# Sums of weight blocks at the start of a Winograd-form product: GpSimd arithmetic replaced by ScalarE negations and accumulating DMAs

## The reference, cut to what matters

```python
# x: (128, 64, 1024); all float32
h   = gelu(cond @ W0 + b0); h = gelu(h @ W1 + b1)
att = softmax(h @ W2 + b2)                                   # (128, 8)
y   = einsum('boi,bih->boh', einsum('bk,koi->boi', att, weight), x) + (att @ bias_k)[:, :, None]
base   = einsum('bsd,od->bso', y, base_W)                    # (1024, 1024) weights
probs  = softmax(einsum('bsd,ed->bse', y, router_W))         # 8 experts, top 2, renormalised
mid    = einsum('bsd,edr->bser', y, lora_A) * w_dense[..., None]
out    = x + base + einsum('bser,erd->bsd', mid, lora_B) * 2
```

## Time and profile before

| | |
|---|---|
| time, median of 3 (lowest, highest) | 975.08 us (975.04, 975.86) |
| profiled execution's own time | 974.32 us |
| span of its instructions | 972.6 us |
| TensorE busy | 953.3 us |
| VectorE busy | 762.2 us |
| ScalarE busy | 231.6 us |
| GpSimd busy | 328.1 us |
| mean granted TensorE clock | 0.995 of full |

### The profile page before, as it was taken

How to read it: one execution, slowest core, us unless ns; L and a number is a source line. 1 busy time by engine, 2 the same in 40 slices (tenths; PEclk the granted TensorE clock), 3 DMA queues, 4 the chain that set the end, 5 groups by cost and what they waited for, 6 DMA issues and landing times.

```text
span 972.6 us, 17914 instructions
## 1 busy us (share of the span) xinstructions
PE 953.3 (98%) x5747; PEld 878.0 (90%) x5747; DVE 762.2 (78%) x1650; ACT 231.6 (24%) x537; POOL 328.1 (34%) x247
## 2 busy tenths in 40 slices
PE   8789999999999999999999999999999999999998
PEld 6679999999999999999999999999999999999996
DVE  6998787777787777787777787777787777787774
ACT  4442222221222221222221222221222221222210
POOL 5833313333313333312333312333312333312331
PEclk9989999999999999999999999999999999999999
DMA  8243433323433323433323433323432323433311
GB/s 302 71 136 93 136 112 111 109 96 113 135 110 111 117 88 113 135 112 109 114 91 113 135 113 108 124 81 113 135 117 104 119 86 113 135 118 103 129 48 47
DMA packets 45969, 110.73 MB, mean 114 GB/s; under 512 B 20352, under 2 KB 20480, under 8 KB 45440
## 3 DMA queue, kind: packets, MB, share of 16 engines
q1 hardware_dynamic: 45680, 110.49, 34.8%
q10 hardware_dynamic: 272, 0.03, 0.0%
HBM read 76.92 MB, written 33.59 MB: 114 GB/s over the span
## 4 chain that ended last, share of the span: by engine, by line
PE 94%; DVE 5%; issue 1%; ACT 0%; POOL 0%; DVEq 0%; POOLq 0%; ACTq 0%
PE pc L511 17%; PE pa L522 13%; PE pb L522 13%; PE y_ps L483 11%; PE pb L525 10%; PE pa L525 10%; PE pd L511 9%; PE pd L566 4%; PE pc L566 4%; DVE w_lo L901 1%; PE pd L548 1%; PE pd L556 1%; DVE a_lo L997 0%; DVE b_lo L1123 0%; DVE ya L988 0%
## 5 line engine op out<-in xcount | busy, mean ns | idle before, releaser
L420 POOL TENSOR_TENSOR out_sb<-out_sb,u 128x512 f32<-128x512 f32 x93 | 132.1, 1449 | 208.4 <-DVE u L1083 208.4
L483 PE MATMUL y_ps<-mix_w,x_sb 128*128 128x128 f32 x1024 | 194.6, 274 | 0.2
L483 PEld LDWEIGHTS y_ps<-mix_w,x_sb 128*128 128x128 f32 x1024 | 167.8, 190 | 13.1 <-DVE ya L988 0.8
L390 POOL TENSOR_TENSOR ya<-ya 128x512 f32<-128x512 f32 x31 | 42.2, 1361 | 400.3 <-DVE ya L988 400.3
L988 DVE TENSOR_TENSOR ya<-y_ps,bias_sb 128x512 f32<-128x512 f32 x128 | 87.8, 686 | 35.6 <-PE y_ps L483 31.6
L511 PE MATMUL pc<-w_hi,s_hi 128*128 128x512 f32 x248 | 102.4, 413 | 0.0
L522 PE MATMUL pa<-w_hi,a_hi 128*128 128x376 f32 x248 | 97.8, 394 | 0.7 <-ACT p L821 0.7
L511 PE MATMUL pc<-w_hi,s_lo 128*128 128x512 f32 x248 | 97.5, 393 | 0.0
L511 PE MATMUL pc<-w_lo,s_hi 128*128 128x512 f32 x248 | 96.9, 391 | 0.0
L813 ACT ACTIVATE mid_hi<-pd 128x128 fp32r<-128x128 f32 x64 | 17.8, 278 | 282.7 <-PE pd L556 282.7
L806 ACT ACTIVATE exps<-logits,neg_max 128x8 f32<-128x8 f32 x64 | 19.3, 301 | 271.7 <-DVE neg_max L1005 271.7
(11 more groups left out here) (218 smaller groups left out, 2567.1 us busy)
## 6 DMA issues: line engine op xcount, KB each, us to landing
x_sb<-in_x SPq DMA_DIRECT2D x64, 512.0 KB, 3.9
out_sb<-in_x SPq DMA_DIRECT2D x64, 512.0 KB, 4.4
out<-out_sb SPq DMA_DIRECT2D x64, 512.0 KB, 2.7
bias_sb<-bias_rows SPq DMA_DIRECT2D x62, 64.0 KB, 4.8
a_raw<-in_base_t SPq DMA_DIRECT2D x1, 1024.0 KB, 7.6
b_raw<-in_base_t SPq DMA_DIRECT2D x1, 1024.0 KB, 11.9
c_raw<-in_base_t SPq DMA_DIRECT2D x1, 1024.0 KB, 13.0
w_raw<-in_base_t SPq DMA_DIRECT2D x1, 1024.0 KB, 14.8
```

The lines of the kernel that those rows point to most:

```text
L390: nc.gpsimd.tensor_tensor(y_block(0, 1), y_block(0, 1), y_block(0, 0), ALU.subtract).then_inc(s3_set, 1)
L420: nc.gpsimd.tensor_tensor(o, o, u2[:, :], ALU.add).then_inc(done, 1)
L483: mm = nc.tensor.matmul(y_ps[q % 2][:, j * P:(j + 1) * P], x_sb[m][:, c * P:(c + 1) * P], mix_w[m][:, :], start=True, stop=True)
```

## The change

B11 and B21 are loaded straight into the places of T2 and T4 in `w_raw`, and B12 is loaded two more times, into the places of T3 and T1, by two further 1 MiB loads in SyncE's queue ahead of `lora_b`. ScalarE writes the negative of a block into one of two buffers `neg[0]`, `neg[1]` (each 1 MiB, over the space of the operands S3, S2 and S1, S4), in two pieces of 128x1024, and a DMA issued by GpSimd adds the buffer to the block (`add_to`, `accum_op=ALU.add`): T3 = B12 + (-B22), T1 = B12 + (-B11), T2 = B11 + (-T3), T4 = B21 + (-T2). Each such DMA moves 1 MiB from SBUF to SBUF. Eight ScalarE negations of 128x1024 are added, the 16 GpSimd instructions go. `neg[0]` holds -B11 and then -T3, `neg[1]` -B22 and then -T2, so each buffer is written anew only after the add that read it. The lists of ScalarE and VectorE in `first_pair` are put in another order: T3's low part after the negation of T3; S3's high and low parts, T1's and T2's parts later; VectorE's waits for T1, T3 and T2 ahead of B12's and B22's low parts go. In ScalarE's list `exponents(0)` comes ahead of the wait for T3, and `exponents(1)` stands behind the waits for T3 and T1. GpSimd's `sum_s3` stands behind the add into T2, and `sum_s2` behind that into T4.

The diff, without the removal of three helpers and one constant that nothing else uses:

```diff
@@ -122,8 +121,9 @@
         lb_raw = over("lb_raw", D, lb_lo_at)
-        a_raw = over("a_raw", BLOCK, op_at[S3])
-        b_raw = over("b_raw", BLOCK, op_at[S1])
+        a_raw = w_raw[:, T2 * BLOCK:(T2 + 1) * BLOCK]
+        b_raw = w_raw[:, T4 * BLOCK:(T4 + 1) * BLOCK]
+        neg = [over(f"neg{n}", BLOCK, op_at[o]) for n, o in enumerate((S3, S1))]
         c_raw = over("c_raw", BLOCK, out_at[1])
...
@@ -166,7 +166,9 @@
             "params_in", "mix_i_in", "bk_in", "side_in", "lb_in"))
-        a_in, b_in, c_in, d_in = (sem(n) for n in ("a_in", "b_in", "c_in", "d_in"))
+        a_in, b_in, c_in, d_in, t1_in, t3_in = (sem(n) for n in ("a_in", "b_in", "c_in", "d_in", "t1_in", "t3_in"))
+        neg_b11_set, neg_b22_set, neg_t3_set, neg_t2_set = (sem(n) for n in (
+            "neg_b11_set", "neg_b22_set", "neg_t3_set", "neg_t2_set"))
         zeros_set, consts_set, pick_set = sem("zeros_set"), sem("consts_set"), sem("pick_set")
...
@@ -261,13 +259,15 @@
             sp.dma_start(bk_sb[:, :], bias_k).then_inc(bk_in, 16)
-            sp.dma_start(a_raw[:, :], base_t[0, :, :]).then_inc(a_in, 16)
+            sp.dma_start(a_raw, base_t[0, :, :]).then_inc(a_in, 16)
             sp.dma_start(x_sb[0][:, :], x_t[0, :, :]).then_inc(x_in[0], 16)
...
             sp.dma_start(x_sb[1][:, :], x_t[1, :, :]).then_inc(x_in[1], 16)
-            sp.dma_start(b_raw[:, :], base_t[2, :, :]).then_inc(b_in, 16)
+            sp.dma_start(b_raw, base_t[2, :, :]).then_inc(b_in, 16)
             sp.dma_start(c_raw[:, :], base_t[1, :, :]).then_inc(c_in, 16)
             sp.dma_start(d_raw, base_t[3, :, :]).then_inc(d_in, 16)
+            sp.dma_start(w_raw[w_block(T3)], base_t[1, :, :]).then_inc(t3_in, 16)
+            sp.dma_start(w_raw[w_block(T1)], base_t[1, :, :]).then_inc(t1_in, 16)
             sp.dma_start(lb_raw[:, :], lora_b.rearrange("e r d -> (e r) d")).then_inc(lb_in, 16)
...
@@ -348,41 +348,15 @@
             for n in range(WP):
-                nc.gpsimd.tensor_copy(w_hi[w_piece(B11, n)], a_raw[half_block(n)]).then_inc(w_hi_set[B11], 1)
+                nc.gpsimd.tensor_copy(w_hi[w_piece(B11, n)], w_raw[w_piece(T2, n)]).then_inc(w_hi_set[B11], 1)
             for n in range(WP):
                 pool.wait_ge(w_hi_set[B11], n + 1)
-                nc.gpsimd.tensor_tensor(w_lo[w_piece(B11, n)], a_raw[half_block(n)],
+                nc.gpsimd.tensor_tensor(w_lo[w_piece(B11, n)], w_raw[w_piece(T2, n)],
                                         w_hi[w_piece(B11, n)].bitcast(f32), ALU.subtract).then_inc(w_lo_set[B11], 1)
 
-            def make_t1(n):
-                nc.gpsimd.tensor_tensor(w_raw[t_piece(T1, n)], c_raw[quarter(n)], a_raw[quarter(n)],
-                                        ALU.subtract).then_inc(t1_made, 1)
-
-            def make_t3(n):
-                nc.gpsimd.tensor_tensor(w_raw[t_piece(T3, n)], c_raw[quarter(n)], w_raw[t_piece(B22, n)],
-                                        ALU.subtract).then_inc(t3_made, 1)
-
-            def make_t2(n):
-                pool.wait_ge(t1_made, n + 1)
-                nc.gpsimd.tensor_tensor(w_raw[t_piece(T2, n)], w_raw[t_piece(B22, n)], w_raw[t_piece(T1, n)],
-                                        ALU.subtract).then_inc(t2_made, 1)
-
-            def make_t4(n):
-                pool.wait_ge(t2_made, n + 1)
-                nc.gpsimd.tensor_tensor(w_raw[t_piece(T4, n)], b_raw[quarter(n)], w_raw[t_piece(T2, n)],
-                                        ALU.subtract).then_inc(t4_made, 1)
-
-            pool.wait_ge(c_in, 16)
-            for n in range(TP):
-                make_t1(n)
-            pool.wait_ge(d_in, 16)
-            for n in range(TP):
-                make_t3(n)
-            for n in range(TP):
-                make_t2(n)
-            pool.wait_ge(b_in, 16)
-            for n in range(TP):
-                make_t4(n)
+            def add_to(blk, of, done):
+
+                nc.gpsimd.dma_start(w_raw[w_block(blk)], neg[of][:, :], accum_op=ALU.add).then_inc(done, 16)
 
...
@@ -420,7 +394,19 @@
             def first_pair():
+                pool.wait_ge(t3_in, 16)
+                pool.wait_ge(neg_b22_set, WP)
+                add_to(T3, 1, t3_made)
+                pool.wait_ge(t1_in, 16)
+                pool.wait_ge(neg_b11_set, WP)
+                add_to(T1, 0, t1_made)
+                pool.wait_ge(w_lo_set[B11], WP)
+                pool.wait_ge(neg_t3_set, WP)
+                add_to(T2, 0, t2_made)
                 sum_s3(1)
+                pool.wait_ge(w_lo_set[B21], WP)
+                pool.wait_ge(neg_t2_set, WP)
+                add_to(T4, 1, t4_made)
                 sum_s2(1)
...
@@ -746,8 +732,14 @@
 
-                nc.scalar.activation(w_hi[w_piece(blk, n)], b_raw[half_block(n)] if blk == B21 else
-                                     w_raw[w_piece(blk, n)], ACT.Copy).then_inc(w_hi_set[blk], 1)
+                nc.scalar.activation(w_hi[w_piece(blk, n)], w_raw[w_piece(T4 if blk == B21 else blk, n)],
+                                     ACT.Copy).then_inc(w_hi_set[blk], 1)
+
+            def negate(blk, to, done):
+
+                for n in range(WP):
+                    nc.scalar.activation(neg[to][half_block(n)], w_raw[w_piece(blk, n)], ACT.Copy,
+                                         scale=-1.0).then_inc(done, 1)
 
...
@@ -825,6 +817,8 @@
                 nc.scalar.copy(att_rows[:, :], pb[:, BANK:]).then_inc(att_rows_set, 1)
+                act.wait_ge(a_in, 16)
+                negate(T2, 0, neg_b11_set)
                 split_high(A12, 0, y_ready, 4)
...
@@ -836,35 +830,37 @@
                     take_hi(B22, n)
+                negate(B22, 1, neg_b22_set)
                 for m in range(2):
...
                 nc.scalar.activation(lb_hi[:, :], lb_raw[:, :], ACT.Copy).then_inc(lb_hi_set, 1)
-                act.wait_ge(t3_made, TP)
+                exponents(0)
+                act.wait_ge(t3_made, 16)
                 for n in range(WP):
                     take_hi(T3, n)
-                exponents(0)
-                for n in range(WP):
-                    take_hi(T1, n)
+                act.wait_ge(t1_made, 16)
+                negate(T3, 0, neg_t3_set)
                 exponents(1)
...
                 split_mid(0, None, 0)
-                act.wait_ge(t2_made, TP)
                 for n in range(WP):
-                    take_hi(T2, n)
+                    take_hi(T1, n)
                 split_high(A11, 1, y_ready, 6)
                 split_mid(1, plain_up, 2)
-                act.wait_ge(w_lo_set[B11], WP)
-                split_high(S3, 1, s3_set, 1)
                 split_high(A12, 1, y_ready, 8)
...
                     place_mix(2, m)
+                act.wait_ge(t2_made, 16)
+                negate(T2, 1, neg_t2_set)
+                split_high(S3, 1, s3_set, 1)
+                for n in range(WP):
+                    take_hi(T2, n)
 
...
                 if second(p):
-                    act.wait_ge(t4_made, TP)
-                    act.wait_ge(w_lo_set[B21], WP)
+                    act.wait_ge(t4_made, 16)
                 split_high(S1, p, s1_set, p)
...
@@ -898,9 +894,8 @@
                 dve.wait_ge(w_hi_set[blk], n + 1)
-                nc.vector.tensor_tensor(w_lo[w_piece(blk, n)], b_raw[half_block(n)] if blk == B21 else
-                                        w_raw[w_piece(blk, n)], w_hi[w_piece(blk, n)].bitcast(f32),
-                                        ALU.subtract).then_inc(w_lo_set[blk], 1)
+                nc.vector.tensor_tensor(w_lo[w_piece(blk, n)], w_raw[w_piece(T4 if blk == B21 else blk, n)],
+                                        w_hi[w_piece(blk, n)].bitcast(f32), ALU.subtract).then_inc(w_lo_set[blk], 1)
 
...
@@ -1116,8 +1111,6 @@
                     sum_mix(1, m, scaled)
-                dve.wait_ge(t1_made, TP)
-                dve.wait_ge(t3_made, TP)
                 for n in range(WP):
...
@@ -1126,7 +1119,7 @@
                 route_weigh(0, pa[:, SMID])
-                dve.wait_ge(t2_made, TP)
+                dve.wait_ge(neg_b22_set, WP)
                 for n in range(WP):
...
@@ -1139,8 +1132,6 @@
                 add_bias(1, 1)
-                for n in range(WP):
-                    take_lo(T3, n)
                 split_low(A11, 1)
...
@@ -1148,21 +1139,24 @@
                 add_into(0, 0, 1, pc[:, :], plain_out)
-                split_low(S3, 1)
+                dve.wait_ge(neg_t3_set, WP)
+                for n in range(WP):
+                    take_lo(T3, n)
                 add_bias(1, 3)
-                for n in range(WP):
-                    take_lo(T1, n)
                 split_low(A12, 1)
...
                     sum_mix(2, m, scaled)
-                dve.wait_ge(t4_made, TP)
+                split_low(S3, 1)
                 for n in range(WP):
-                    take_lo(T2, n)
+                    take_lo(T1, n)
                 dve.wait_ge(res_in[0][1], 16)
...
                 add_into(0, 1, 1, pd[:, :], plain_out)
```

(11 more changed lines are left out.)

## The result

| | before | after |
|---|---|---|
| median | 975.65 us | 978.59 us |
| lowest, highest | 975.04, 976.65 | 977.48, 978.69 |
| profiled execution, span | 972.6 us | 975.7 us |

The ratio is 1.003, with a 95% interval of 1.0021 to 1.0039: slower by 0.3%. The forecast was 978.4 us. The profiled execution after took 977.48 us, against 977.6 in the working. The total came out as forecast, but by two errors that cancel each other, and behind a gain on offer of 12 us.

What follows compares the result with a forecast made beforehand. TensorE bounds the kernel, idling early for VectorE, which GpSimd's sums slow. After new waits for the adds, +0.3 and +3.0 for low clock give +3.3: 974.3 + 3.3 = 977.6, median 978.4 us, range 969.5 to 988.

Steps and rivals of the forecast that it cites:

- What the removal gives: Start of the kernel without GpSimd's sums: first up-projection could start at 42.2 instead of 52.99, 10.8 us free.
- Step 1: First two adds, into T3 and T1: T3's issued at 29.8, T1 landing at 29.8 + T + X + Q = 44.5.
- T: Time of an accumulating DMA from issue on GpSimd to landing: 7.0 us, with 0.5 for the issue.
- X: Time by which a second queued accumulating DMA lands after the first: 5.1 us.
- Step 2: New first wait, at the up-projection behind T1's landing: start at 48.3 instead of 42.2, TensorE idle 6.1 us.
- Step 3: From the up-projection's start to T4's add: 14.0 us on VectorE and ScalarE, T4's add issued at 62.3.
- Step 4: New second wait, `keep_p1` queued behind T4: second product at 72.6 instead of 72.33, TensorE idle some 6 us.
- Step 5: Low clock after the second wait, from 72.6: 6.1 us at 0.50 costs 3.0 us.
- (a): Rival: adds as cheap as copies, T 4.0, X 2.6, second product at 64.1, total 969.9 us; chance 0.27.
- (b): Rival: within 0.2%, T from 5.2 to 6.5, between one read and two, 973.1 to 977.0 us; chance 0.20.
- (c): Rival: clearly slower, write and reads take turns or descriptors take microseconds, T 9.6, X 7.7, 986.2 us; chance 0.21.
- (d): Rival: VectorE is slow at the start for another reason and stays so, +8 to +12 us; chance 0.04.

Runs made afterwards that it cites:

- memset kernel: Kernel before, with the 16 GpSimd subtractions that make T1 to T4 replaced by memsets of the same tiles: 963.1 us, ratio 0.9876.
- held kernel: Kernel after, with SyncE waiting for T4's landing before it loads the residual of the second pair: 977.01 us, ratio 1.002.
- copying kernel: Kernel after, with `accum_op` left out so that the same four DMAs copy instead of add: 971.1 us, ratio 0.996.
- last kernel: Kernel after with lists reordered, operand sums and mixing weights moved, and SyncE waiting for T4 before the second pair's residual: 967.3 us, ratio 0.9915.
- first reordering: Kernel after, same instructions and DMAs, ScalarE and VectorE lists reordered so that what needs no sum precedes the waits: 971.58 us, ratio 0.9962.
- move of the operand sums: On the first reordering: S2, S1, S4 sums ahead of T4's add on GpSimd, a bias addition and `make_u2` earlier: 971.44 us, ratio 0.9965.
- two steps behind it: On the move of the operand sums: SyncE held before the third pair's residual and mixing weights later, 970.0 us; then held before the second pair's, 967.3 us.

## Why the prediction held, point by point

**What the removal gives** was right. B21's low parts at 23.81 (forecast 23.2), `mid` at 33.58 (33.3), no wait over 1 us before 40; the last product ahead of the up-projection ends at 42.7 (42.2). The memset kernel puts the whole gain at 12.2 us.

**Step 1.** T3's add is issued at 31.03, not 29.8: the negation of B22 came 0.6 later, and GpSimd's issue another 0.6 behind it. T was right (7.4 against 7.0), X too (5.4 against 5.1). Of the 7.0, the 0.5 us for GpSimd's issue came from no row of before; the issue of a single add took 0.85 us. Q, the backlog of the loads that I let fall on the adds with 2.6 us, was close to zero: in 32 to 44 us 175 GB/s are 2.1 MB, and the two adds alone are that much. The DMA share of 1.02 from 20 to 25 us and of 0.70 from 28 to 31 shows that the two added loads had run in the space before. T1 landed at 43.8 (44.5): an issue 1.2 later, T and X together 0.7 longer, and a backlog 2.6 smaller.

**Step 2.** The wait is there, at L560, for `mid_lo`, and 4.7 us long; I had 6.1. What is queued behind T1's landing was named rightly, and moving it moved the wait.

**Step 3.** From T1's landing to T4's issue 18.7 us, against 17.8 in my list of single steps. The issue itself is right only because 0.7 early and 0.9 long cancel: 62.5 (62.3).

**Step 4** is the mis-sized term. I priced T4's add like T3's, at 7.0 us. It took 8.3, since stores and residual loads share the engines from 62 to 71 us (share 1.00). The held kernel shows 6.9. The second product starts at 74.09 (72.6), after 9.6 us of idling instead of 6, as the product before it was done at 64.5 already: 1.8 us behind the kernel before, where I had 0.3. The DMA traffic that I did charge, Q, was at the adds that had the engines to themselves, and none at the one that had not.

**Step 5** erred the other way. I took 3.0 us for the low clock from one stretch of before. After the 9.6 us wait TensorE had only 3.2 us of it (0.52 from 74.0 to 77.2), and from the second product to A22·T4 were 16.9 us instead of 15.5: 1.4 us.

**Sum.** +1.8 + 1.4 is +3.2 (measured 3.1), against +0.3 + 3.0 = +3.3. The mechanisms and both waits were right; the total to a tenth was luck, as the two errors of about 1.5 us have opposite signs.

**The rivals.** (a) fell: an add isn't as cheap as a copy. The copying kernel is its case, 4.2 us below before where it had 5.2, but with a T4 that took 8.6 us and not 4.0. (b) asked for T under 6.5, and no add was seen under 6.9. (c) fell too, though T4's add took its 9.8 to 11.9 us in other orders. (d) is out by the memset kernel.

**What stays open.** How much of the last kernel's gain belongs to each of its moves was separated only in part: against the kernel after, 7.0 us came with the first reordering, 0.1 with the move of the operand sums, 1.4 and 2.7 with the two steps behind it. What the 2.5 us wait for the mixing weights costs was not tried. Whether such an order of the lists, with the sums left on GpSimd, would gain by itself was not tried.

## What to carry to other kernels

An instruction that waits for a DMA holds up all that stands behind it on its engine: put in front of it what others need and what does not depend on it, step by step, since the wait moves to the next thing left behind (4.7 us at one place became 5.2 at the next). Price an accumulating DMA at a little over twice the copy's time in a queue (5.4 against 2.4 us for 1 MiB here), plus what shares the engines during it, and look at that very stretch. Taking 12 us of contention away gave a loss of 3 in one order of the lists and a gain of 8.4 in another (with two loads held back as well), so when an engine is relieved, the order around it is part of the change.

## What the runs showed of the hardware that was not expected

- The accumulating DMA of 1 MiB within SBUF took 6.9 to 7.7 us from issue to landing with nothing or little beside it (T3 in every order, T4 where the transfers were held back), 7.4 to 8.5 with one load of 0.5 MiB beside it (T2), and 8.3 to 11.9 beside stores and residual loads (T4). A plain copy took 4.5 to 5.1 alone and 7.0 to 8.6 beside them.
- TensorE worked at low clock for 5.4 us after a wait of 4.7 us, but only for 3.2 us after one of 9.6. The trace shows where the rest went: in the longer wait the granted clock was 0.50 from 67 us on, so 7 us of the low stretch passed while TensorE stood idle; in the shorter one it was 0.68 from 46 to 47 us and then 0.50, less than 1.5 us before the work resumed at 47.6. The low clock cost less after the longer wait. What sets its whole length is not settled.
- GpSimd's issue of a single accumulating DMA takes 0.85 to 0.88 us, that of the same DMA as a copy 0.53 to 0.57.
- GpSimd instructions that only write leave VectorE alone (2.36 us for the pair), one-input reads cost it about a third (3.0 to 3.2), two-input reads 60 to over 100% (3.8 to 4.9).
